# A graph layer that gathers its node rows: one tile of sixteen is picked by TensorE from rows kept in SBUF

## Chip, cores and metric

The kernel runs on one core of one Trainium2 chip. The metric is the device time of one execution in microseconds (us), here the median of three runs. The profile is of one further execution.

## What is computed

The program is two layers of a graph network over 8192 nodes of 128 f32 values and 262,144 edges sorted by `dst`, each layer followed by a residual sum and a layer norm. The change lies in the second layer, in which each edge takes the row of its source node, multiplies it with its nine attributes in a tensor product with fixed coefficients and learned weights, and is summed into its target node:

```python
x = _layernorm(x + _L0_gnn_ref(x, src, dst, edge_weight, L0_gnn_W))
# second layer, edge_index = (src, dst), edge_attr = edge_attr_9 (262144, 9)
summand = _tensor_product(x[src], edge_attr, [w0, w1, w2, w3, w4])   # (262144, 128)
out = segment_sum(summand, dst, num_segments=8192) / sqrt(10.0)
x = _layernorm(x + out)
```

## The kernel before

After the first layer and its norm the node rows lie in DRAM as `x1`. The second layer (`layer1`) walks the edges in 128 rows of 16 tiles of 128 edges. Each engine has a program of its own, written out by hand, and they meet at semaphores.

- **POOL** (GpSimd) gathers: for each tile one indirect DMA fetches the 128 source rows of `x1` into `feat[z][:, t, :]`, edge by edge on the partitions. `feat` has two slots of a row each (`ROW_SLOTS` is 2), and each slot two halves of 8 tiles; before a half of row r is gathered POOL waits until PE has used that half of row r - 2 (`half_summed`).
- **DVE** (VectorE) makes `attr_hot` for row r + 2 in row r (`next_hots`, `hots`): a comparison of a ramp (`iota`) with the target nodes gives a one-hot of 16 nodes for each edge, and a product with the nine attributes 9 x 16 columns for each tile. The one-hot and the ramp lie in PSUM in a corner of `y` (`loop_hot`, `loop_iota`) for rows 0 to 113; the one-hots made in rows 112 to 125, for which `y` is needed otherwise, use `late_hot` and the constants in SBUF. DVE also adds `quad` into `group` (`add_quads`, half by half) and the mixed sums into `g.acc` (`add_pair`).
- **PE** (TensorE) multiplies, in `half_row`, 8 tiles of `feat` with their `attr_hot` into the PSUM tile `quad`; after every second row `mix` applies the weights to `group` (nine products of 384 columns). Products of f32 operands show as two matmul records each. `turn_attr` turns the attributes of the next 8 rows (an octet) onto the edges' partitions.
- **ACT** (ScalarE) clears `quad` and `group`, copies the turned attributes and casts the indices. **SP** loads attributes.

Rows 0 to 7 stand in a first piece, 8 to 111 in a loop over octets, and 112 to 127 are written out, since in 112 to 126 the finished batches of 512 nodes are also turned (`turn_nodes`), summed with `x1`, measured and normalized (`measure`, `normalize`) and stored. The last batch follows behind row 127.

The order in one row of the loop is this on DVE (names as in the code below):

```python
add_quads(w, r, n, j // 2 % 2, j % 2, 0, offs)
if starts:
    add_pair(n - 1, starts)
add_quads(w, r, n, j // 2 % 2, j % 2, 1, offs)
next_hots(o, j)
```

Of the kernel before, what the change touches and what calls it, by code (L numbers as in the profile page):

```python
# [36 lines left out]
P = 128  # L37
# [7 lines left out]
TABLES = 1  # L45
# [47 lines left out]
START_LAG = 3  # L93
BATCH = 4
# [84 lines left out]
def gnn_kernel(nc, x, src, dst, attr, weight, w_lin, w_tp, consts, out, tables, x1):  # L179
# [10 lines left out]
    with ExitStack() as ctx:  # L190
# [31 lines left out]
        layer1(nc, g, x1, attr, out)  # L222
# [1197 lines left out]
def layer1(nc, g, x1, attr, out):  # L1420
# [5 lines left out]
    with ExitStack() as ctx:  # L1426
# [6 lines left out]
        off_f = sb("off_f", [P, TN], F32)  # L1433
        tile_offs = sb("tile_offs", [P, TN // Q, Q - 1], I32)
# [6 lines left out]
        late_hot = sb("late_hot", [P, R, WIN], F32)  # L1441
# [8 lines left out]
        x_t = [sb(f"x_t{i}", [P, BATCH, D], F32) for i in range(2)]  # L1450
        z_t = [sb(f"z_t{i}", [P, BATCH, D], F32) for i in range(2)]
        x_last = sb("x_last", [P, BATCH, D], F32)
        z_last = sb("z_last", [P, BATCH, D], F32)
# [6 lines left out]
        LOOPED = EARLY // O  # L1460

# [21 lines left out]
        x_used = sem("x_used")  # L1483
        y_made = sem("y_made")
# [23 lines left out]
        def in_slot(w, e):  # L1508

            return w * ((NE + 1 - e % 2) // 2) + e // 2  # L1510

# [8 lines left out]
        def _(sp):  # L1520
# [7 lines left out]
            sp.wait_ge(attr_turned, 2)  # L1528
            load_attr(1)

            def load_x(w, e):

                sp.wait_ge(x_used, w * NE + max(e + 1, 2))
                sp.dma_start(x_t[e % 2][:], batches(x1)[e]).then_inc(x_here[e % 2], 16)

            sp.dma_start(x_last[:], batches(x1)[NE]).then_inc(x_last_here, 16)
            with passes(sp) as w:
                with sp.Fori(0, LOOPED) as o:
                    sp.wait_ge(attr_turned, w * (2 * OCTETS) + o * 2 + 4)
                    load_attr(o + 2)  # L1540
                load_x(w, 0)
                for r in range(EARLY, RN):
                    if r % O == TURN_ROW + 1:
                        sp.wait_ge(attr_turned, w * (2 * OCTETS) + (r // O * 2 + 4))
# [3 lines left out]
            n_loads = sp.value_load(g.n_pass[0:1, 1:2], min_val=1, max_val=g.PASSES1)  # L1548
            sp.wait_ge(attr_here, n_loads * (16 * OCTETS) + 32)
# [3 lines left out]
        def _(pool):  # L1553
            with passes(pool) as w:
                with pool.Fori(0, OCTETS) as o:  # L1555
                    for j in range(O):
                        z = j % S
                        if j % (O // 2) == 0:
                            pool.wait_ge(ids_made, w * (2 * OCTETS) + o * 2 + (j // (O // 2) + 1))  # L1559
                        for h in range(2):  # L1560
                            pool.wait_ge(half_summed, summed(w, o * O, (j - S) * 2 + h))  # L1561
                            pool.sem_inc(g.turn, 1)  # L1562
                            for t in range(h * H, h * H + H):
                                c = j % (O // 2) * R + t
                                pool.indirect_dma_start(  # L1565
                                    feat[z][:, t, :], None, x1,
                                    bass.IndirectOffsetOnAxis(ap=ids[j // (O // 2)][:, c:c + 1], axis=0),
                                ).then_inc(feat_in[z][h], 16)
                for z in range(S):
                    for h in range(2):  # L1570
# [442 lines left out]
```

## Time and profile before

| | |
|---|---|
| median of 3 runs | 4139.94 us (4139.83 to 4140.0) |
| profiled execution, its own time | 4139.79 us |
| its span, first to last instruction | 4138.0 us |
| busy: PE / DVE / ACT / POOL | 2400.2 / 2119.9 / 1420.4 / 2769.7 us |
| gathers of the second layer (L1565) | 2048, 1960.3 us busy, mean 957 ns |
| mean granted TensorE clock | 0.749 |

The busy time of an engine is the sum of its instructions; "idle before" is the time in which the engine did nothing ahead of them, with what ended it. "issue" is idle time that nothing in the profile explains. L1565 is line 1565 of the kernel. A granted clock of 1.00 is 2.4 GHz, of 0.50 is 1.2 GHz.

### The profile page before, as it was taken

What the parts mean: (1) busy time and instruction counts of PE and PEld (TensorE: products, weight loads), DVE (VectorE), ACT (ScalarE), POOL (GpSimd) and SP (SyncE); (2) the same over time, 40 slices, a digit from 0 to 9 for tenths busy, and PEclk for the clock granted to TensorE, in tenths of its full rate; (3) what the DMA queues carried; (4) which work ended last, traced back from release to release, by engine and by line L of the source; (5) the groups of instructions that cost most, each with busy time, mean ns of one, the idle gap of its engine ahead of it and who ended that gap; (6) DMA issues with size and microseconds to landing.
All of it is one profiled execution on the core that took longest, in us unless ns stands there. A gap on an engine that the chain in (4) does not pass through costs nothing.

```text
span 4138.0 us, 55255 instructions
## 1 busy us (share of the span) xinstructions
PE 2400.2 (58%) x15332; PEld 2126.9 (51%) x15334; DVE 2119.9 (51%) x4357; ACT 1420.4 (34%) x2142; POOL 2769.7 (67%) x2887
## 2 busy tenths in 40 slices
PE   2200199999999964555455554545555455555454
PEld 1000199999999954444444444444444444444443
DVE  8999888888888872232222332322332222323433
ACT  5444366666666651121121211211121111212222
POOL 5100077777777737777777777777777777777775
PEclk6555599999999966677776776767667766776767
DMA  1000133333333332221221222222221221212222
GB/s 58 8 0 20 63 97 96 97 96 98 96 96 92 96 115 59 53 59 53 58 58 53 58 58 53 58 58 53 58 58 53 58 58 52 58 53 73 79 75 57
DMA packets 116447, 268.24 MB, mean 65 GB/s; under 512 B 50449, under 2 KB 50593, under 8 KB 115233
## 3 DMA queue, kind: packets, MB, share of 16 engines
q0 software_dynamic: 92080, 191.02, 17.4%
q1 hardware_dynamic: 19698, 68.09, 4.7%
q10 hardware_dynamic: 4608, 8.39, 0.5%
q8 instruction: 28, 0.46, 0.0%
q14 instruction: 33, 0.27, 0.0%
HBM read 252.30 MB, written 8.72 MB: 63 GB/s over the span
## 4 chain that ended last, share of the span: by engine, by line
POOL 42%; issue 16%; PE 4%; DMA 1%; POOLq 0%; DVE 0%; ACT 0%; DVEq 0%
POOL feat L1565 42%; PE quad L1730 3%; PE mixed L1742 1%; DMA feat<-x,ids 1%; POOLq L1561 0%; POOLq L1562 0%; PE attr_t L1690 0%; ACT z_last L1669 0%; DVE group L1878 0%; DVE dst_col L1965 0%; POOLq L1555 0%; DVE z_last L1976 0%; DVE stats L1979 0%; PE y L1754 0%; POOLq L1559 0%
## 5 line engine op out<-in xcount | busy, mean ns | idle before, releaser
L1565 POOL DMA_INDIRECT feat<-x,ids x2048 | 1960.3, 957 | 636.3 <-issue 632.3
L1730 PE MATMUL quad<-attr_hot,feat 128*128 128x144 f32 x4096 | 919.8, 407 | 1229.4 <-DMA feat<-x,ids 644.3
L1730 PEld LDWEIGHTS quad<-attr_hot,feat 128*128 128x128 f32 x4096 | 860.5, 294 | 1292.9 <-issue 1286.6
L1878 DVE TENSOR_TENSOR group<-group,quad 128x504 f32 (+1 forms) x512 | 347.9, 679 | 1725.5 <-PE quad L1730 1681.5
L1137 POOL DMA_INDIRECT l_feat<-in_x,id_of x768 | 727.7, 948 | 601.7 <-ACT w_of L830 366.4
L1582 ACT ACTIVATE quad<-quad 128x1008 uint32<-128x1008 uint32 x258 | 256.6, 995 | 1834.0 <-DVE group L1878 1834.0
L1742 PE MATMUL mixed<-group,mix 128*128 128x384 f32 x1152 | 414.9, 518 | 17.9 <-DVE group L1878 17.9
L1039 DVE TENSOR_SCALAR keys<-swap,src_of,w_of 128x184 f32<-128x184 f32 x1024 | 327.1, 389 | 93.5 <-PE l_pre L1230 93.5
L1039 DVE TENSOR_SCALAR w_row<-swap,src_of,w_of 128x184 f32<-128x184 f32 x1024 | 327.6, 390 | 51.4 <-PE l_pre L1230 49.7
L1742 PEld LDWEIGHTS mixed<-group,mix 128*128 128x128 f32 x1152 | 235.4, 209 | 171.7 <-issue 49.5
L1211 PE MATMUL got<-x_near,far_w 128*128 128x128 bf16 x4224 | 301.0, 220 | 11.0 <-ACT far_w L847 11.0
L1854 DVE TENSOR_TENSOR attr_hot<-y,attr_e 128x2304 f32<-128x2304 f32 x114 | 291.5, 2557 | 3.9
L1211 PEld LDWEIGHTS got<-x_near,far_w 128*128 128x128 bf16 x4224 | 272.4, 98 | 26.0 <-issue 11.3
L856 ACT COPY pad<-got 128x640 f32<-128x640 f32 x256 | 177.2, 692 | 291.0 <-PE got L1211 245.2
L1586 ACT ACTIVATE group<-group 128x3456 uint32<-128x3456 uint32 x66 | 203.4, 3083 | 193.4 <-PE mixed L1742 193.4
L1230 PE MATMUL l_pre<-keys,pad 128*128 128x184 f32 x1280 | 262.5, 319 | 0.0
L1230 PE MATMUL l_pre<-w_row,pad 128*128 128x184 f32 x1280 | 262.1, 319 | 0.0
L842 ACT ACTIVATE far_keys<-place,turn_f 128x384 bf16<-128x384 bf16 (+2 forms) x384 | 229.4, 631 | 7.0 <-DMA place<-table 6.9
L1230 PEld LDWEIGHTS l_pre<-keys,pad 128*128 128x128 f32 x1280 | 213.1, 190 | 0.0
L1230 PEld LDWEIGHTS l_pre<-w_row,pad 128*128 128x128 f32 x1280 | 212.6, 190 | 0.0
L1230 PE MATMUL l_pre<-keys,l_feat 128*128 128x184 f32 x768 | 189.9, 329 | 0.0
L1230 PE MATMUL l_pre<-w_row,l_feat 128*128 128x184 f32 x768 | 189.4, 328 | 0.0
(252 smaller groups left out, 2428.7 us busy)
## 6 DMA issues: line engine op xcount, KB each, us to landing
place<-table SPq DMA_DIRECT2D x64, 640.0 KB
feat<-x,ids POOLq DMA_INDIRECT x2048, 2.5
l_feat<-in_x,id_of POOLq DMA_INDIRECT x768
attr_in<-in_edge_attr SPq DMA_DIRECT2D x18, 576.0 KB, 3.8
norm_x<-in_x SPq DMA_DIRECT2D x16, 256.0 KB, 2.7
x<-norm_z ACTq DMA_DIRECT2D x16, 256.0 KB, 2.4
x_t<-x SPq DMA_DIRECT2D x15, 256.0 KB, 2.7
out<-z_t ACTq DMA_DIRECT2D x15, 256.0 KB, 2.1
```

What stands on the lines that cost most here:

```text
L842: nc.scalar.activation(rest_far[r][:, cols[r]], placed_at(s, j, cols[r]), ACT.Abs, bias=not_wanted[r]).then_inc(far_made, 2 // len(cols))
L1039: made = nc.vector.tensor_scalar(hot_of[(j % 2) * GROUP + i], iota[KIND[j][i]], src_of[s % 2][:, c:c + 1], w_of[s % 2][:, c:c + 1], ALU.is ...
L1137: pool.indirect_dma_start(feat[:, landing, :], None, x, bass.IndirectOffsetOnAxis(ap=id_of[s % 2][:, c:c + 1], axis=0)).then_inc(feat_in[l ...
L1211: last = nc.tensor.matmul(got[z][:, cols], hot, rows, start=(n_done == 0), stop=(n_done == len(products) - 1))
L1230: made = nc.tensor.matmul(pre[:, s % 2, bass.ds(places[i], WIN0)], rows, hot_of[(j % 2) * GROUP + i], start=False, stop=(j == GROUPS - 1 a ...
L1565: pool.indirect_dma_start(feat[z][:, t, :], None, x1, bass.IndirectOffsetOnAxis(ap=ids[j // (O // 2)][:, c:c + 1], axis=0),).then_inc(feat ...
L1582: nc.scalar.memzero(quad[:, 2 * h:2 * h + 2, 0:NA * QUAD_WIN]).then_inc(quad_zero, 1)
L1586: nc.scalar.memzero(group[n % 2][:]).then_inc(group_zero, 1)
L1730: last = nc.tensor.matmul(bank[:, :, bass.ds(places[t % H], WIN)], feat[z % S][:, t, :], attr_hot[z % 2][:, t, :, :], start=False, stop=(t ...
L1742: last = nc.tensor.matmul(to, g.mix[:, m, :], group[side][:, m, :, :], start=(m == 0), stop=(m == NA - 1))
L1854: nc.vector.tensor_tensor(attr_hot[z][:], hot.unsqueeze(2).to_broadcast(s4), by_tile.unsqueeze(3).to_broadcast(s4), ALU.mult).then_inc(hot ...
L1878: nc.vector.tensor_tensor(to, to, quad[:, q, 0:NA * QUAD_WIN].rearrange("p (m n) -> p m n", m=NA), ALU.add).then_inc(quad_added, 1)
```

## The change

In rows 16 to 112 tile 15 of each row is no longer gathered; POOL issues 8 gathers for the first half and 7 for the second. Its 128 node rows are picked on the chip:

- In rows 0 to 7 all node rows of `x1` are loaded in 16 batches and split into three bf16 parts whose sum is the f32 value, which stay in SBUF (`x3`, 64 blocks of 128 nodes x 3 x 128). ACT makes a part by a cast (`split_part`), PE subtracts it in PSUM with an identity and a negated identity (`keep_left`).
- Before row 0 DVE writes two numbers for each edge of the 128 last tiles (`src` modulo 128, and its block plus 1), which SP stores and then, four rows ahead, loads row by row onto all partitions (`load_codes`).
- In row r DVE compares them for the tile of row r + 2: `shift_codes` (four operations of 128 columns) and `block_hots`, two bursts of 8 comparisons of 512 bf16 columns each, which write `pick_hot`, a one-hot of 64 blocks x 128 edges.
- PE multiplies the 64 blocks of `pick_hot` with the 64 blocks of `x3` in `pick`, 32 behind each half of a row, into 384 columns of `y` (`picked`); DVE sums the three parts into tile 15 of the row after (`take_picked`).
- The one-hots of the edges and their ramp get a PSUM bank of their own (`hots_at`) for all rows; `attr_t` shrinks from two banks to one, so the attributes are turned in three steps, not two. `late_hot`, `z_t`, `x_last` and `z_last` go; the batches are normalized in `x_t`, which lies in the memory of `pick_hot`.

```diff
-        late_hot = sb("late_hot", [P, R, WIN], F32)
...
-        attr_t = ctx.enter_context(nc.psum_tensor("attr_t", [P, 2, 512], F32))
+        attr_t = ctx.enter_context(nc.psum_tensor("attr_t", [P, O // 2 * P], F32))
...
-        loop_hot = y[:, 0:R * WIN].rearrange("p (t n) -> p t n", t=R)
-        loop_iota = y[:, R * WIN:R * WIN + WIN]
...
+        hots_at = ctx.enter_context(nc.psum_tensor("hots_at", [P, 512], F32))
+        hot = hots_at[:, 0:R * WIN].rearrange("p (t n) -> p t n", t=R)
+        iota = hots_at[:, R * WIN:R * WIN + WIN]
...
+        x3 = sb("x3", [P, NODE_BLOCKS, 3, D], BF16)
+        pick_hot = sb("pick_hot", [P, NODE_BLOCKS, P], BF16)
+        code4 = sb("code4", [P, HOT_BLOCKS, P], BF16)
...
+        picked = y[:, 0:3 * D]
...
+        PICK = 2 * O
+        PICKS = EARLY + 1 - PICK
+        CODED = PICKS + 1
...
+            def load_codes(w, r, s):
+
+                sp.wait_ge(codes_used, coded(w, r - PICK) + 1)
+                sp.sem_inc(g.turn, 1)
+                sp.dma_start(codes_at[:, s, :], rows[bass.ds(r, 1)].to_broadcast([P, P])).then_inc(codes_here[s], 16)
...
+                    for h in range(2):
+                        pool.wait_ge(half_summed, summed(w, o * O, (j - S) * 2 + h))
+                        pool.sem_inc(g.turn, 1)
+                        for t in range(h * H, h * H + (second if h else H)):
+                            c = j % (O // 2) * R + t
+                            pool.indirect_dma_start(
+                                feat[z][:, t, :], None, x1,
+                                bass.IndirectOffsetOnAxis(ap=ids[j // (O // 2)][:, c:c + 1], axis=0),
+                            ).then_inc(feat_in[z][h], 16)
...
+                with pool.Fori(2, LOOPED) as o:
+                    for j in range(O):
+                        gather_row(o, j, H - 1)
+                for r in range(EARLY, RN):
+                    gather_row(r // O, r % O, second_half(r))
...
+            def split_part(w, b, part):
+
+                if part == 0:
+                    act.wait_ge(x_here[b % 2], split_load(w, b) * 16 + 16)
+                    rows = x_t[b % 2]
+                else:
+                    act.wait_ge(left_made, w * (2 * g.NB) + (2 * b + part))
+                    rows = y[:].rearrange("p (a d) -> p a d", a=BATCH)
+                nc.scalar.copy(x3[:, b * BATCH:(b + 1) * BATCH, part, :], rows).then_inc(split, 1)
...
+            def keep_left(w, b):
+
+                rows = y[:].rearrange("p (a d) -> p a d", a=BATCH)
+                for part in range(2):
+                    pe.wait_ge(split, w * (3 * g.NB) + (3 * b + part + 1))
+                    if part == 0:
+                        nc.tensor.matmul(rows, g.cst[:, C_IDENT:C_IDENT + P], x_t[b % 2], start=True, stop=False,
+                                         skip_group_check=True)
+                    nc.tensor.matmul(rows, minus, x3[:, b * BATCH:(b + 1) * BATCH, part, :], start=False, stop=True,
+                                     skip_group_check=True).then_inc(left_made, 1)
+
+            def pick(w, k, half):
+
+                pe.wait_ge(pick_hots, coded(w, k) * 2 + (half + 1))
+                if half == 0:
+                    pe.wait_ge(pick_out, picks_done(w, k) + 1)
+                pe.sem_inc(g.turn, 1)
+                for b in range(half * (NODE_BLOCKS // 2), (half + 1) * (NODE_BLOCKS // 2)):
+                    last = nc.tensor.matmul(picked, pick_hot[:, b, :], x3[:, b, :, :].rearrange("p c d -> p (c d)"),
+                                            start=(b == 0), stop=(b == NODE_BLOCKS - 1), skip_group_check=True)
+                last.then_inc(pick_made, 1)
...
+                if with_pick is not None:
+                    pe.wait_ge(pick_out, picks_done(w, with_pick) + 2)
...
+                    half_row(w, r, 0, j, fills * H)
+                    turn_rest(w * OCTETS + o + 1, j)
+                    if first:
+                        keep_left(w, 2 * j)
+                    if pick_next:
+                        pick(w, r - (PICK - 1), 0)
+                    half_row(w, r, 1, j, n_second, r - PICK if with_pick else None)
+                    if first:
+                        keep_left(w, 2 * j + 1)
+                    if pick_next:
+                        pick(w, r - (PICK - 1), 1)
...
+            def shift_codes(w, i, s, n_slot):
+
+                dve.wait_ge(codes_here[s], n_slot * 16 + 16)
+                nc.vector.scalar_tensor_tensor(code4[:, 0, :], codes[:, s, 0, :], g.cst[:, C_PLACE:C_PLACE + 1],
+                                               codes[:, s, 1, :], ALU.is_equal, ALU.mult).then_inc(codes_used, 1)
+                dve.wait_ge(codes_used, coded(w, i) + (CODE_SLOTS + 1))
+                for k in range(1, HOT_BLOCKS):
+                    nc.vector.tensor_scalar(code4[:, k, :], code4[:, 0, :], float(k), None,
+                                            ALU.subtract).then_inc(code_shifted, 1)
+                dve.wait_ge(code_shifted, coded(w, i) * (HOT_BLOCKS - 1) + (HOT_BLOCKS - 1))
+
+            def block_hots(half):
+
+                n = NODE_BLOCKS // 2 // HOT_BLOCKS
+                for b in range(half * n, (half + 1) * n):
+                    made = nc.vector.tensor_scalar(pick_hot[:, b * HOT_BLOCKS:(b + 1) * HOT_BLOCKS, :], code4[:],
+                                                   float(b * HOT_BLOCKS + 1), None, ALU.is_equal)
+                made.then_inc(pick_hots, 1)
+
+            def take_picked(w, k, z):
+
+                dve.wait_ge(pick_made, picks_done(w, k) * 2 + 2)
+                nc.vector.tensor_reduce(feat[z][:, R - 1, :], picked.rearrange("p (c d) -> p d c", c=3), AX_X,
+                                        ALU.add).then_inc(pick_out, 1)
...
+                    if code_next:
+                        i = r - (PICK - 2)
+                        s = (j + 2) % CODE_SLOTS
+                        n_slot = coded_in_slot(w, s) + o * (O // CODE_SLOTS) + ((j + 2) // CODE_SLOTS - PICK // CODE_SLOTS)
+                        dve.wait_ge(split, (w + 1) * (3 * g.NB))
+                        if take_next:
+                            dve.wait_ge(pick_made, picks_done(w, r - (PICK - 1)) * 2 + 1)
+                        shift_codes(w, i, s, n_slot)
+                        block_hots(0)
                     add_quads(w, r, n, j // 2 % 2, j % 2, 1, offs)
                     next_hots(o, j)
+                    if take_next:
+                        take_picked(w, r - (PICK - 1), (j + 1) % S)
+                    if code_next:
+                        block_hots(1)
```

The diff leaves out the loads and stores around the codes, the table work before row 0, and the late rows. Two places show how the engines' programs read now. The first is DVE in one row of the loop; before, from the first half's adds (L1878) to the one-hots of row r + 2:

```order
L1878 TENSOR_TENSOR group<-group,quad 128x9x56
L1871 REGISTER_ALU
L1874 REGISTER_ALU
...
L1878 TENSOR_TENSOR group<-group,quad 128x9x56
L1849 REGISTER_ALU
L1850 TENSOR_TENSOR y<-y,dst_col 128x256
L1854 TENSOR_TENSOR attr_hot<-y,attr_e 128x2304
L1859 TENSOR_LOAD row_offs
```

And of the change at the same place (L2075 are the adds, L2090 and L2094 the codes' shifts, L2102 the bursts, L2109 the sum of the parts; `code` is `code4`, and `tile_start` holds the codes):

```order
L2075 TENSOR_TENSOR group<-group,quad 128x9x56
...
L2090 SCALAR_TENSOR_TENSOR code<-tile_start,cst 128x128
L2094 TENSOR_SCALAR code<-code 128x128 x3
L2102 TENSOR_SCALAR pick_hot<-code 128x512 x8
L2068 REGISTER_ALU
...
L2075 TENSOR_TENSOR group<-group,quad 128x9x56
L2047 TENSOR_TENSOR hots_at<-hots_at,dst_col 128x256
L2051 TENSOR_TENSOR attr_hot<-hots_at,attr_e 128x2304
L2108 REGISTER_ALU
L2109 TENSOR_REDUCE feat<-y 128x128
L2102 TENSOR_SCALAR pick_hot<-code 128x512 x8
```

The first burst now stands between the two halves' adds, the second behind the one-hots.

The second place is PE in the same rows; before, from the last tile of a first half (L1730) to the first of the second:

```order
L1730 MATMUL quad<-attr_hot,feat 128x9x16
L1713 ISA
L1713 TENSOR_LOAD tile_offs
L1723 REGISTER_ALU
L1730 MATMUL quad<-attr_hot,feat 128x9x16
```

And of the change, where the quad matmuls are L1900 and the pick is L1883 (`x` is `x3`):

```order
L1900 MATMUL quad<-attr_hot,feat 128x9x16
L1878 ISA
L1880 ISA
L1883 MATMUL y<-x,pick_hot 128x384 x32
L1859 ISA
L1859 TENSOR_LOAD tile_start
L1891 REGISTER_ALU
```

Between the halves, and behind the second one in the same way, 32 matmuls of the pick now stand in PE's program.

## Rows read from the trace of the kernel before

**Rows 1.** Page, part 2: busy tenths in 40 equal slices of the span

```profile
POOL 5100077777777737777777777777777777777775
```

**Rows 2.** Groups by line, 1600 to 3600 us (count | busy us, mean ns | idle before, releasers)

```profile
L1565 POOL DMA_INDIRECT feat<-x,ids x1602 | 1512.4, 944 | 488.1 <-issue 486.2 <-PE quad L1730 1.8
...
L1878 DVE TENSOR_TENSOR group<-group,quad 128x504 f32 x300 | 203.9, 680 | 926.6 <-PE quad L1730 890.3 <-issue 8.0
...
L1600 ACT COPY attr_e<-attr_t 128x512 f32<-128x512 f32 x26 | 14.0, 589 | 25.2 <-DVE attr_hot L1854 25.2
```

**Rows 3.** Windows, 2000 to 2400 us (busy us of PE, PEld, DVE, ACT, POOL; clock)

```profile
2000.00:2400.00 400.00, 205.48 (x836) 171.66 (x835) 118.35 (x141) 74.08 (x64) 302.51 (x321) 0.70 0.21 56
```

**Rows 4.** Waits of POOL, 1600 to 3600 us (total us, times, longest)

```profile
POOL feat L1565 <- PE quad L1730: 1.8, 6, 0.3
```

**Rows 5.** Timeline, POOL: first and last gather of the layer (start, duration)

```profile
1529.47 2.17 POOL L1565 DMA_INDIRECT feat<-x,ids  x1 [12.63 <-issue]
...
4112.46 0.94 POOL L1565 DMA_INDIRECT feat<-x,ids  x1 [0.30 <-issue]
```

**Rows 6.** Page, part 5: all gathers of the second layer

```profile
L1565 POOL DMA_INDIRECT feat<-x,ids x2048 | 1960.3, 957 | 636.3 <-issue 632.3
```

**Rows 7.** Groups by line, 3810 to 4130 us

```profile
L1565 POOL DMA_INDIRECT feat<-x,ids x226 | 235.7, 1043 | 68.9 <-issue 67.9 <-PE quad L1730 0.6 <-DMA feat<-x,ids 0.3
```

**Rows 8.** Timeline, a late row at 3883 us

```profile
3883.37 2.56 DVE L1854 TENSOR_TENSOR attr_hot<-late_hot,attr_e 128x2304 f32<-128x2304 f32 x1
3883.72 3.03 POOL L1565 DMA_INDIRECT feat<-x,ids  x1 [0.30 <-issue]
```

**Rows 9.** Timeline, the start of the second layer

```profile
1531.94 1.29 POOL L1565 DMA_INDIRECT feat<-x,ids  x1 [0.30 <-issue]
...
1534.04 1.50 DVE L1833 TENSOR_SCALAR off_f<-tile_start,keep 128x2048 f32<-128x2048 f32 x1
1534.79 1.55 POOL L1565 DMA_INDIRECT feat<-x,ids  x1 [0.30 <-issue]
...
1536.65 2.03 POOL L1565 DMA_INDIRECT feat<-x,ids  x1 [0.30 <-issue]
```

**Rows 10.** Timeline, first layer: a burst of comparisons and a gather

```profile
510.95 0.32 DVE L1029 TENSOR_SCALAR far_w<-place,cst 128x384 bf16<-128x384 bf16 x1 [7.11 <-DMA place<-table]
...
511.18 0.31 DVE L1030 TENSOR_SCALAR far_w<-place,cst 128x384 bf16<-128x384 bf16 x1
511.33 0.98 POOL L1137 DMA_INDIRECT l_feat<-in_x,id_of  x1 [0.30 <-issue]
511.41 0.31 DVE L1029 TENSOR_SCALAR far_w<-place,cst 128x384 bf16<-128x384 bf16 x1
511.64 0.31 DVE L1030 TENSOR_SCALAR far_w<-place,cst 128x384 bf16<-128x384 bf16 x1
```

**Rows 11.** Line 1137, gathers of the first layer, 700 to 1400 us (min/median/max ns)

```profile
L1137 POOL DMA_INDIRECT l_feat<-in_x,id_of x560: 940/945/1050, 699.5 to 1399.6; - x187
```

**Rows 12.** Line 1159, f32 matmuls of 512 columns (min/median/max ns)

```profile
L1159 PE MATMUL got<-l_feat,cst x24: 1061/1126/1223, 59.8 to 214.6; 128*128 128x512 f32 x24
```

**Rows 13.** Timeline, PE: half rows and a mix

```profile
1544.05 4.18 PE L1730 MATMUL quad<-attr_hot,feat 128*128 128x144 f32 x16 [5.89 <-DMA feat<-x,ids]
...
1597.60 5.97 PE L1742 MATMUL mixed<-group,mix 128*128 128x384 f32 x18
...
1604.09 2.20 PE L1730 MATMUL quad<-attr_hot,feat 128*128 128x144 f32 x16 [0.41 <-issue]
...
4085.80 2.12 PE L1730 MATMUL quad<-attr_hot,feat 128*128 128x144 f32 x16
```

**Rows 14.** Timeline, first layer, PE: matmuls of 128 bf16 columns

```profile
1005.97 1.00 PE L1211 MATMUL got<-x_near,far_w 128*128 128x128 bf16 x15
...
1006.80 0.22 PE L1211 MATMUL got<-x_rest,far_w 128*128 128x128 bf16 x1
```

**Rows 15.** Windows, first layer, 800 to 900 us

```profile
800.00:900.00 100.00, 100.00 (x1003) 98.43 (x1002) 86.30 (x275) 67.33 (x136) 75.62 (x81) 1.00 0.32 98
```

More of the change, by code:

```diff
@@ L1483, in layer1 @@
         x_used = sem("x_used")
+        src_here = sem("src_here")
+        code_step = sem("code_step")
+        codes_made = sem("codes_made")
+        codes_stored = sem("codes_stored")
+        codes_here = [sem(f"codes_here{s}") for s in range(CODE_SLOTS)]
+        codes_used = sem("codes_used")
+        code_shifted = sem("code_shifted")
+        split = sem("x_split")
+        left_made = sem("x_left_made")
+        pick_hots = sem("pick_hots")
+        pick_made = sem("pick_made")
+        pick_out = sem("pick_out")
         y_made = sem("y_made")
@@ new lines, in _ @@
+                with pool.Fori(0, 2) as o:
+                    for j in range(O):
+                        gather_row(o, j, H)
+                with pool.Fori(2, LOOPED) as o:
+                    for j in range(O):
+                        gather_row(o, j, H - 1)
+                for r in range(EARLY, RN):
+                    gather_row(r // O, r % O, second_half(r))
+                landings = [16 * n for z in range(S) for n in (H * (RN // S), landed_before(RN + z))]
+                for landing, n in zip(sum(feat_in, []), landings):
+                    pool.wait_ge(landing, n)
@@ L1610, in normalize @@
                 for a in range(BATCH):
[L1611 removed]
+                    done = nc.scalar.activation(x_t[e % 2][:, a, :], x_t[e % 2][:, a, :], ACT.Identity,
                                                 bias=shift[:, a:a + 1], scale=rstd[:, a:a + 1])
@@ L1668, in _ @@
             for a in range(BATCH):
-                done = nc.scalar.activation(z_last[:, a, :], z_last[:, a, :], ACT.Identity, bias=shift[:, a:a + 1],
+                done = nc.scalar.activation(x_last[:, a, :], x_last[:, a, :], ACT.Identity, bias=shift[:, a:a + 1],
                                             scale=rstd[:, a:a + 1])
@@ L1689, in turn_attr @@
                 for n, m in enumerate(ms):
-                    last = nc.tensor.transpose(attr_t[:, n // 4, n % 4 * P:(n % 4 + 1) * P], edges[:, :, m],
+                    last = nc.tensor.transpose(attr_t[:, n * P:(n + 1) * P], edges[:, :, m],
                                                g.cst[:, C_IDENT:C_IDENT + P])
@@ L1773, in _ @@
                 pe.wait_ge(landings_cleared, w + 1)
+                pe.wait_ge(x_used, w * NE + 2)
                 pe.sem_inc(g.turn, 1)
                 for j in range(O):
-                    row(0, j, first=True)
-                with pe.Fori(1, LOOPED) as o:
+                    row(0, j, first=True, pick_next=False, with_pick=False)
+                for j in range(O):
+                    row(1, j, pick_next=(j == O - 1), with_pick=False)
+                with pe.Fori(2, LOOPED) as o:
                     for j in range(O):
@@ L1840, in _, with hots @@
             dve.sem_inc(hot_made, 1)
-            def hots(u, r, j, z, late=False):
-                hot = late_hot[:] if late else loop_hot
-                iota = g.cst[:, C_IOTA:C_IOTA + WIN] if late else loop_iota
+            nc.vector.tensor_copy(iota, g.cst[:, C_IOTA:C_IOTA + WIN]).then_inc(iota_made, 1)
+            dve.wait_ge(iota_made, 1)
+            dve.wait_ge(src_here, 16)
+            nc.vector.tensor_scalar(low_i, src_tail, P - 1, None, ALU.bitwise_and).then_inc(code_step, 1)
+            nc.vector.tensor_scalar(block_i, src_tail, 7, NODE_BLOCKS - 1, ALU.logical_shift_right,
+                                    ALU.bitwise_and).then_inc(code_step, 1)
+            dve.wait_ge(code_step, 2)
+            nc.vector.tensor_copy(code_out[:, 0, :], low_i)
+            nc.vector.tensor_copy(block_f, block_i).then_inc(code_step, 1)
+            dve.wait_ge(code_step, 3)
+            nc.vector.tensor_scalar(code_out[:, 1, :], block_f, 1.0, None, ALU.add).then_inc(codes_made, 1)
+            def hots(u, r, j, z):
                 cols = bass.ds(r * R, R)
@@ L1946, in _ @@
                 for j in range(O):
-                    row(0, j, first=True)
-                with dve.Fori(1, LOOPED) as o:
+                    row(0, j, first=True, code_next=False, take_next=False)
+                for j in range(O):
+                    row(1, j, code_next=(j >= O - 2), take_next=(j == O - 1))
+                with dve.Fori(2, LOOPED) as o:
                     for j in range(O):
```

231 lines of the change are left out of this document (148 added, 83 removed).

## Prediction

> **What bounds the kernel now.** I read the page's slices first [rows 1]. The second layer fills the last 25 of the 40 slices; there POOL stands at 7 tenths in all but the last, where the kernel ends. The groups by line over 1600 to 3600 us [rows 2] say what POOL's 7 tenths are: 1602 gathers with 1512.4 us busy and 488.1 us idle before them, which is 2000.5 of 2000 us. So POOL issues one gather every 1.249 us (0.944 busy, 0.305 "issue") without a pause, and a row of 16 takes 19.98 us. The waits [rows 4] confirm that nothing holds it: it waited for PE 6 times, 1.8 us in all. The window [rows 3] shows the room elsewhere: in 400 us, twenty rows, PE is busy 205 us (10.3 a row) and DVE 118 us (5.9 a row), with TensorE granted 0.70 of its clock.
>
> The second layer is therefore one POOL stream. Its first gather starts at 1529.47 and its last ends at 4113.40 [rows 5]; 24.6 us of tail follow to the end of the span at 4138.0. The profiled run took 4139.79 us, 1.8 us more than its span and 0.15 us less than the median of the three runs.
>
> The stream is not quite even. Over all 2048 gathers POOL is busy 1960.3 us [rows 6], against 2048 x 0.944 = 1933.3 at the middle's duration: 27.0 us of lengthened gathers. They lie at the two ends. In the last rows the mean is 1043 ns [rows 7], since a gather that starts under the product for `attr_hot`, which there reads `late_hot` and `attr_e`, both in SBUF, lasts until 0.8 us after that product ends [rows 8] (3883.37 + 2.56 = 3885.93; the gather ends at 3886.75). At the start of the layer single-source work on long SBUF tiles does the same [rows 9] (the scalar product ends at 1535.54, the gather at 1536.34). So a gather needs something that DVE holds, once, some 0.13 us after its start (0.94 - 0.81).
>
> **The change, part by part.**
>
> *Gathers removed.* Rows 16 to 112 are 97 rows with one gather less: 97 x 1.249 = 121.1 us off the stream. The gathers that stay keep their duration and their "issue" gap; nothing in POOL's program between them changes.
>
> *One-hots in their own bank.* The late product now reads its one-hot from PSUM, as the middle rows do, where no gather is longer than 0.95 us. Of the 27.0 us the first gather [rows 5] and three others of the start [rows 9] hold 3.3 (2.17 + 1.29 + 1.55 + 2.03 less 4 x 0.944); 23.7 us remain for the late rows and go. The last 226 gathers alone give 235.7 - 226 x 0.944 = 22.4 [rows 7], and they leave out one of the fourteen rows concerned.
>
> *DVE's one-hots of the nodes.* A row adds two bursts of 8 comparisons, bf16 128x512 from SBUF to SBUF, four small operations before the first burst, and a reduction of 384 PSUM columns. The nearest rows are the first layer's comparisons, 128x384 bf16, which start every 0.23 us in a burst [rows 10]. For 512 columns that is between 0.23 and 0.31; I take 0.27, so 2.1 us a burst, 4.3 a row. With about 0.9 for the small ones and at most 0.68 for the reduction (an add of 504 PSUM columns [rows 2]) DVE goes from 5.9 to about 11.8 us a row, of 18.7. It is not the bound. Behind its waits for the picks stand the second half's adds and the one-hots of row r + 2; PE needs those a row later.
>
> *What the bursts do to the gathers.* A gather that starts amid a burst of four such comparisons took 0.98 us in place of 0.94 [rows 10], and over 700 us of the first layer, with DVE busy some 86% [rows 15] with such short operations, 560 gathers had a median of 945 and a maximum of 1050 ns [rows 11]. So a short comparison delays a gather by its own few hundredths at most, and POOL gets in between two of them. A row has 4.3 / 1.249 = 3.4 gathers under a burst: 3.4 x 0.04 = 0.14 us a row, 13 us in all. The bounds are 0 and, at the maximum of 0.105 each, 35 us.
>
> The Trainium skill has a rule that speaks against this change (SBUF — State Buffer, section "Who interferes with whom"): single-source copies and tensor_scalar operations in SBUF can run in a two-port mode, and then hold the port pair that VectorE shares with GpSimd for the whole instruction, while the other engine is fully blocked. For a long instruction the trace agrees [rows 9]. Taken of a whole burst the rule would give the 4286 us of the second rival below, where the rows of short instructions [rows 10, 11] give 4008.
>
> *PE.* This is the change's real cost. A pick is 64 matmuls of 384 bf16 columns. In the first layer 15 matmuls of 128 bf16 columns, weights loaded anew for each, take 1.00 us [rows 14], one alone 0.22: (1.00 - 0.22) / 14 = 0.056 us each. Three times that is 0.167, and 10.7 us a pick. Half a row of tiles takes 2.12 to 2.20 at the high clock and 4.18 at the low; a mix every second row 5.97 after a half row that had raised the clock [rows 13]. Two rows at the high clock: 4 x 2.12 + 5.97 + 2 x 10.7 + 0.5 of transposes (9 x 128 columns in 8 rows, as many as a half row has) = 36.4 us, against POOL's 2 x 15 x 1.249 = 37.5. PE fits, with 1.1 us to spare in two rows. At the low clock it would need twice that, far beyond POOL. Which level holds? Of the 255 half rows that the trace shows whole, all 63 that began within 0.6 us of earlier PE work ran at the high clock (2.12 to 2.20), while the other 192, after 4.5 us idle or more, began at the low one [rows 13] (the first of each kind, and the last of the 63); and where PE is busy 100% the granted clock is 1.00 (2.4 GHz) for 100 us on end [rows 15]. With PE busy 97% I take the high level.
>
> Do the waits cost PE anything? A half row waits for its gathers, as now. The picks of PE's row r use one-hots that DVE made in row r - 1, and the reduction of the pick before has to be done when a pick begins: when a pick ends DVE may still have the edges' one-hots in hand (2.56 us [rows 8] and a short comparison before it) and then the reduction, while PE has a half row of 2.1 and perhaps a mix to do first, and the adds and one-hots were begun during the pick's 5.3. POOL runs almost two rows ahead of PE (two buffers), so a late PE of a few us costs nothing as long as the average fits.
>
> *Work hidden.* In rows 0 to 7 ACT and PE split the node rows: a half row of tiles (4.18), an identity matmul of 512 f32 columns in two passes of 1.13 [rows 12], three copies of 512 columns (0.59 each, as the copy from `attr_t` [rows 2]) and two bf16 products (0.45 each: 4 x 0.056, doubled for the low clock) follow each other: about 4.2 + 2.3 + 1.8 + 0.9 = 9.2 us a half row of POOL's 10.0. With a mix every second row (3.0 a row) that is 21.4 against 20.0: a lag of at most 1.4 us a row, 11 over eight rows. It lies under POOL's lead, since POOL needs half a buffer back only 24 gathers (30 us) after it filled it; without that cover it would cost the 11 us. On SP the next octet's attributes now stand behind the codes' loads, which wait until DVE has used a slot four rows before; the attributes are wanted several rows later still, and the third turning of them lies between PE's waits. None of this touches POOL's queue.
>
> **Sum**, against the profile's own span: 4138.0 - 121.1 - 23.7 + 13 = 4006.2 us; with the 1.8 around it **4008 us**, 3.2% faster. Its own range is 3990 to 4040 (the gathers' bounds are 3995 and 4030).
>
> **Rivals.**
> *PE becomes the bound.* For it: only 1.1 us of room in two rows, and no row shows a restart after 0.6 to 4.5 us of idle time, which is just what PE will have. Against it: a PE that is late has no gap, so its clock stays up; the loss limits itself. If each gap cost a cold start of 4.18 - 2.12 = 2.06 us, two rows would take 36.4 + 2 x 2.06 = 40.5, as long as now, and the 121 us would be lost. Half way lies 4008 + 60 = **4070 us**. A DVE that waits for PE and PE for it in turn would look alike.
>
> *The bursts starve POOL: slower.* If a burst of back-to-back comparisons held a gather until its end, each burst of 2.1 us would catch one gather, 0.62 us in on average, and delay it by 1.5 us: 3.0 a row, 291 us in 97 rows, less the 13 in the sum: **4286 us**. It decides from 0.75 us a burst on, where the gain (1.249 a row and 23.7 / 97 = 0.24) is eaten. For it: one long instruction does just that [rows 8, 9]. Against it: the gather at 511.33 would then have ended near 512.75, and ended at 512.31 [rows 10].
>
> *The late rows keep their stalls*, since other work of those rows (the batches' normalization) holds the gathers: 4008 + 24 = **4032 us**. Against it: a late gather ends 0.82 us after the product [rows 8], which explains its length whole.
>
> **Chances.** Forecast (3990 to 4040) 0.70; late stalls stay 0.05; PE or DVE bound 0.16, evenly from 4030 to 4135; starved POOL, slower, 0.06; something else 0.03. Up to 4080 about 0.83 is held, so the range is 3990 to 4080. A measurement of this kernel tells about 0.2% (8 us) from no change. Faster by more: 0.89; within it, the far end of PE as the bound: 0.03; slower: 0.08.
>
> **What would show it.** POOL 1951 gathers, still one every 1.25 us, mean near 0.95, waits for PE below 10 us; 18.7 to 18.9 us a row between rows 16 and 112; PE above 90% busy there at a clock near 1.0; no gather of 3 us in the late rows. POOL waiting for PE's half rows, or a clock near 0.7 in that stretch, means the first rival; gathers of 2 us beside the bursts, the second. The prediction is wrong if a pick matmul takes more than 0.18 us in a stream, or if a gather beside a burst loses more than 0.1.

## The result, and the profile after

The changed kernel takes **4013.07 us** (median of 4 runs, 4010.54 to 4014.28) against 4139.89 us before: a ratio of 0.9693, 95% interval 0.9678 to 0.9709, 3.1% faster. The forecast was 4008 us, range 3990 to 4080. The profiled execution took 4012.53 us, its span 4010.7.

From the page of the changed kernel, the share of each engine, the slices of PE, DVE, POOL and TensorE's granted clock, and the costliest groups of the second layer (L1668 are now the gathers, L1883 the pick, L2102 the bursts):

```profile
PE 3135.9 (78%) x21605; PEld 2469.3 (62%) x21606; DVE 2613.2 (65%) x6420; ACT 1446.3 (36%) x2190; POOL 2671.5 (67%) x2790
...
PE   2100189999999995657999999999999999998555
...
DVE  8999878888888874225565555555555555655443
...
POOL 5100077777777756777777777777777777777775
PEclk6555599999999986868999999999999999999777
...
L1668 POOL DMA_INDIRECT feat<-x,ids x1951 | 1862.3, 955 | 606.9 <-issue 585.5
...
L2102 DVE TENSOR_SCALAR pick_hot<-code 128x512 bf16<-128x512 bf16 x1568 | 371.9, 307 | 3.4
```

POOL's row of sevens is the one of [rows 1]: the second layer is still one stream of gathers, 97 fewer. PE has gone from half its time (205 of 400 us, [rows 3]) to 9 tenths without becoming the bound, and its granted clock has risen from 0.70 to 0.99 in these rows.

The groups of the picked rows, 1900 to 3600 us, answer to [rows 2]:

```profile
L1668 POOL DMA_INDIRECT feat<-x,ids x1350 | 1289.5, 955 | 411.4 <-issue 392.5 <-PE quad L1900 18.9
...
L1900 PE MATMUL quad<-attr_hot,feat 128*128 128x144 f32 x2880 | 395.9, 292 | 109.8 <-DMA feat<-x,ids 87.8 <-issue 22.0
```

1350 gathers are 90 rows of 15, so a row takes 1700 / 90 = 18.89 us, and a gather 1.259 where 1.249 was forecast. POOL's busy and idle time add up to 1700.9 us. The 18.9 us put down to PE are the usual gap between two gathers and no hold: POOL's waits for PE in these rows (us in total, times, longest) are at most 0.3 us long.

```profile
POOL feat L1668 <- PE quad L1900: 18.9, 62, 0.3
```

PE's half rows wait for gathers (87.8 us): POOL leads, PE follows.

Two windows of 400 us (busy us of PE, PEld, DVE, ACT, POOL; clock; DMA share) answer to [rows 3]:

```profile
1900.00:2300.00 400.00, 374.29 (x2238) 257.03 (x2238) 231.38 (x596) 77.75 (x69) 303.30 (x318) 0.99 0.24 61
...
3100.00:3500.00 400.00, 373.96 (x2262) 257.44 (x2261) 233.22 (x602) 78.74 (x70) 303.40 (x318) 1.00 0.24 61
```

PE is busy 94%, 17.7 us of a row's 18.89, at 2.4 GHz nearly throughout. The timeline shows one burst, its gathers, a half row and a pick:

```profile
2504.91 0.94 POOL L1668 DMA_INDIRECT feat<-x,ids  x1 [0.30 <-issue]
...
2505.41 1.89 DVE L2102 TENSOR_SCALAR pick_hot<-code 128x512 bf16<-128x512 bf16 x8
2506.16 1.02 POOL L1668 DMA_INDIRECT feat<-x,ids  x1 [0.30 <-issue]
...
2506.29 2.20 PE L1900 MATMUL quad<-attr_hot,feat 128*128 128x144 f32 x16 [1.39 <-DMA feat<-x,ids]
2507.49 0.94 POOL L1668 DMA_INDIRECT feat<-x,ids  x1 [0.30 <-issue]
...
2508.32 5.36 PE L1883 MATMUL y<-x,pick_hot 128*128 128x384 bf16 x32
```

The gather at 2506.16 starts under a burst and takes 1.02 us; the one after it takes 0.94 again. The gather at 2504.91 started before the burst and isn't lengthened, though the burst begins while it runs. PE's half row begins after 1.39 us of idle time and still runs at the high clock (2.20 us; 4.18 at the low one, [rows 13]).

At the two ends of the layer, the first gathers and the last, the last mix, and the group of the late rows, 3690 to 4010 us, which answers to [rows 7]:

```profile
1528.12 1.88 POOL L1668 DMA_INDIRECT feat<-x,ids  x1 [12.62 <-issue]
1530.30 1.56 POOL L1668 DMA_INDIRECT feat<-x,ids  x1 [0.30 <-issue]
1532.16 2.03 POOL L1668 DMA_INDIRECT feat<-x,ids  x1 [0.30 <-issue]
1534.50 2.48 POOL L1668 DMA_INDIRECT feat<-x,ids  x1 [0.30 <-issue]
...
3983.75 0.94 POOL L1668 DMA_INDIRECT feat<-x,ids  x1 [0.30 <-issue]
...
3992.49 7.74 PE L1912 MATMUL mixed<-group,mix 128*128 128x384 f32 x18 [1.99 <-DVE group L2075]
...
L1668 POOL DMA_INDIRECT feat<-x,ids x237 | 223.6, 943 | 72.2 <-issue 71.6 <-PE quad L1900 0.6
```

No late gather is lengthened any more: a mean of 943 ns where it was 1043, and the longest takes 961.

### The profile page after: what moved, and what is told of

It reads as the page before. It is cut to its first block, busy times and chain, and to the rows that moved or that the text cites. A ratio compares the mean times of both kernels' runs of the same rounds, so it can differ in the third digit from the quotient of the medians.

```text
span 4010.7 us, 71536 instructions
## 1 busy us (share of the span) xinstructions
PE 3135.9 (78%) x21605; PEld 2469.3 (62%) x21606; DVE 2613.2 (65%) x6420; ACT 1446.3 (36%) x2190; POOL 2671.5 (67%) x2790
## 4 chain that ended last, share of the span: by engine, by line
POOL 40%; issue 14%; PE 4%; DMA 3%; POOLq 0%; DVE 0%; ACT 0%; DVEq 0%
POOL feat L1668 40%; PE quad L1900 4%; DMA feat<-x,ids 3%; PE mixed L1912 0%; POOLq L1664 0%; POOLq L1665 0%; ACT pick_hot L1807 0%; DVE group L2075 0%; DVE dst_col L2199 0%; POOLq L1676 0%; PE attr_t L1829 0%; DVE pick_hot L2210 0%; DVE stats L2213 0%; DVE acc L2084 0%; POOLq L1574 0%
## 5 line engine op out<-in xcount | busy, mean ns | idle before, releaser
L1668 POOL DMA_INDIRECT feat<-x,ids x1951 | 1862.3, 955 | 606.9 <-issue 585.5
L1883 PE MATMUL y<-x,pick_hot 128*128 128x384 bf16 x6208 | 1044.3, 327 | 0.0
L1900 PE MATMUL quad<-attr_hot,feat 128*128 128x144 f32 x4096 | 643.9, 318 | 353.5 <-DMA feat<-x,ids 184.1
L1900 PEld LDWEIGHTS quad<-attr_hot,feat 128*128 128x128 f32 x4096 | 606.1, 216 | 413.0 <-issue 398.8
L1883 PEld LDWEIGHTS y<-x,pick_hot 128*128 128x128 bf16 x6208 | 609.2, 98 | 383.6 <-issue 3.9
L2075 DVE TENSOR_TENSOR group<-group,quad 128x504 f32 (+1 forms) x512 | 347.3, 678 | 735.3 <-PE quad L1900 698.8
L1912 PE MATMUL mixed<-group,mix 128*128 128x384 f32 x1152 | 395.1, 499 | 16.1 <-DVE group L2075 16.1
L2102 DVE TENSOR_SCALAR pick_hot<-code 128x512 bf16<-128x512 bf16 x1568 | 371.9, 307 | 3.4
L2051 DVE TENSOR_TENSOR attr_hot<-hots_at,attr_e 128x2304 f32<-128x2304 f32 x128 | 327.3, 2557 | 4.4
L1912 PEld LDWEIGHTS mixed<-group,mix 128*128 128x128 f32 x1152 | 222.7, 196 | 163.9 <-issue 30.2
L2090 DVE SCALAR_TENSOR_TENSOR code<-tile_start,cst 128x128 bf16<-128x128 bf16 x98 | 34.5, 352 | 331.8 <-PE y L1883 328.8
```

What stands on the lines that cost most here:

```text
L1668: pool.indirect_dma_start(feat[z][:, t, :], None, x1, bass.IndirectOffsetOnAxis(ap=ids[j // (O // 2)][:, c:c + 1], axis=0),).then_inc(feat ...
L1883: last = nc.tensor.matmul(picked, pick_hot[:, b, :], x3[:, b, :, :].rearrange("p c d -> p (c d)"), start=(b == 0), stop=(b == NODE_BLOCKS ...
L1900: last = nc.tensor.matmul(bank[:, :, bass.ds(places[t % H], WIN)], feat[z % S][:, t, :], attr_hot[z % 2][:, t, :, :], start=False, stop=(t ...
L1912: last = nc.tensor.matmul(to, g.mix[:, m, :], group[side][:, m, :, :], start=(m == 0), stop=(m == NA - 1))
L2051: nc.vector.tensor_tensor(attr_hot[z][:], hot.unsqueeze(2).to_broadcast(s4), by_tile.unsqueeze(3).to_broadcast(s4), ALU.mult).then_inc(hot ...
L2075: nc.vector.tensor_tensor(to, to, quad[:, q, 0:NA * QUAD_WIN].rearrange("p (m n) -> p m n", m=NA), ALU.add).then_inc(quad_added, 1)
```

## The experiments

Eleven kernels ran. Each is compared with the kernel before on its own chip; there that one took 4138.81 us (the bank, no bursts, less work for PE), 4141.85 (the doubled bursts, the two with more work for PE, the codes in PSUM) and 4139.51 (the last four). Except where said, an edit is to the changed kernel.

**The bank without the pick.** All gathers are back, nothing is picked; the split of the node rows and the one-hots' own bank stay.

```diff
-            return H - 1 if PICK <= r < PICK + PICKS else H
+            return H
...
-                def row(o, j, first=False, code_next=True, take_next=True):
+                def row(o, j, first=False, code_next=False, take_next=False):
```

> The one-hots in their own bank and the split of the node rows stay; nothing is picked, so all 2048 tiles are gathered and the codes are neither loaded nor shifted. My account: the late rows' lengthened gathers go and nothing else changes: the time before less 23.7 us, 4116 us (4112 to 4120), and gathers of the late rows at a mean of 944 to 950 ns. If other work of the late rows holds the gathers, 4135 to 4140 us and a mean near 1043 ns there. If the split of the node rows costs POOL time, above 4120 us, with POOL waiting for PE in rows 0 to 9.

Measured: 4116.33 us (ratio 0.9945, 0.9928 to 0.9962). Its gathers between 3800 and 4090 us:

```profile
L1660 POOL DMA_INDIRECT feat<-x,ids x232 | 218.9, 944 | 70.7 <-issue 70.1 <-PE quad L1892 0.6
```

The bank alone gives 22 to 24 us, all of the 23.7 put down to the late rows, so the split of the node rows, which is in this kernel too, costs nothing that can be measured; POOL's waits for PE in its second layer are at most 0.3 us long. The picks account for the other 4116.3 - 4013.1 = 103 us.

**The picks without the bursts.** `pick_hot` is made for the first picked row only.

```diff
+                if again:
+                    dve.sem_inc(pick_hots, 1)
+                    return
```

> The two bursts of comparisons are run for the first picked row alone; in the other 96 rows PE multiplies with the same one-hots, so that tile 15 of these rows gets the nodes of row 16 (left out: the one-hots of rows 17 to 112). PE's work and the gathers are the same. My account: the 16 us by which gathers beside bursts are longer go, 4013 - 16 = 3997 us (3994 to 4000), and the gathers of these rows have a mean of 944 to 946 ns. If the lengthening comes of DVE's other work (the edges' one-hots, the adds): 4011 to 4014 us. If the chain of DVE's bursts and PE's picks sets the row: also below 4000, but with the gathers' mean unchanged and fewer waits of POOL for PE.

Measured: 3996.79 us (0.9657, 0.9641 to 0.9673). The gathers from 1900 to 3600 us:

```profile
L1668 POOL DMA_INDIRECT feat<-x,ids x1362 | 1285.8, 944 | 415.1 <-issue 397.1 <-PE quad L1900 18.0
```

So the bursts cost 4013.1 - 3996.8 = 16.3 us (15 by the two ratios), and the gathers' own duration holds all of it: 11 ns x 15 x 97 = 16.

**The bursts doubled.** Each comparison is issued a second time.

```diff
+                for again in range(2):
+                    for b in range(half * n, (half + 1) * n):
...
+                    if not again:
+                        made.then_inc(hots_once, 1)
+                        dve.wait_ge(hots_once, i * 2 + (half + 1))
```

> Each burst of 8 comparisons is issued twice, the second time behind a wait for the first; DVE goes from 10.9 to about 14.6 us a row. Without bursts the time was 3996.8 us, with them 4013.1, so they cost 16.3. My account (a gather amid short comparisons loses what is left of one, some 0.085 us, however long the burst): twice the cost, 4013 + 16 = 4029 us (4024 to 4036), and a mean of the gathers near 966 ns in rows 16 to 112. If a burst holds a gather until it ends: each burst of 3.8 us catches one gather and delays it by about 3.2 us where it now delays it by 1.3, far above 4150 us. If the chain of DVE and PE sets the row: POOL waits for PE, up to 4013 + 97 x 3.7 = 4370 us.

Measured: 4037.14 us (0.9749, 0.9733 to 0.9765), one us above the range. The gathers from 1900 to 3600 us, and the timeline of one doubled burst:

```profile
L1669 POOL DMA_INDIRECT feat<-x,ids x1334 | 1294.5, 970 | 406.6 <-issue 386.4 <-PE quad L1901 20.1
...
2506.86 3.88 DVE L2104 TENSOR_SCALAR pick_hot<-code 128x512 bf16<-128x512 bf16 x16
2506.93 1.04 POOL L1669 DMA_INDIRECT feat<-x,ids  x1 [0.30 <-issue]
2508.28 1.03 POOL L1669 DMA_INDIRECT feat<-x,ids  x1 [0.30 <-issue]
2509.61 1.02 POOL L1669 DMA_INDIRECT feat<-x,ids  x1 [0.30 <-issue]
2510.93 0.94 POOL L1669 DMA_INDIRECT feat<-x,ids  x1 [0.30 <-issue]
```

Three gathers lie under it, each about 0.09 us longer, and none waits for the burst's end; that ends the starvation rival. The bursts' cost went from 16 to about 37 us (4037.1 - 3996.8, less the 3.0 by which the kernel before ran longer on this chip; by the means 26 ns x 15 x 97 = 38), more than double. The timelines show why: between 1900 and 3600 us 192 of 1350 gathers took 0.97 us or more (hits) in the changed kernel, 2.13 a row, and 423 of 1334 here, 4.76 a row; a hit costs 0.080 there and 0.083 here. The price of a hit is constant, their number grew a little faster than the bursts.

**Less work for PE.** The pick leaves out the third part.

```diff
-        picked = y[:, 0:3 * D]
+        picked = y[:, 0:2 * D]
```

> PE picks two of the three parts, 256 columns a matmul instead of 384 (left out: the third part, so a picked row has 16 bits of its value's 24). That takes 64 x 0.054 = 3.5 us a row from PE. My account: POOL's stream sets the row, so nothing moves: 4013 us (4010 to 4016). If PE sets it: the row falls to POOL's own 15 x 1.249 = 18.74 us, 0.15 us less, 3998 us. If the longer pauses let the clock fall to its low level: half rows of 4.2 us and matmuls of 0.22 us, PE at 7.3 x 2 + 14 = 28 us a row, far above 4100 us, unless the clock comes back.

Measured: 4017.1 us (0.9707, 0.9691 to 0.9723), one us above the range. Its window, and its gathers from 1900 to 3600 us:

```profile
1900.00:2300.00 400.00, 330.38 (x2236) 278.55 (x2237) 228.71 (x597) 77.76 (x69) 303.39 (x318) 0.92 0.23 61
...
L1668 POOL DMA_INDIRECT feat<-x,ids x1347 | 1289.7, 957 | 410.5 <-issue 393.4 <-PE quad L1900 17.1
```

With a third less pick PE's busy time falls by 44 of 374 us, and nothing is gained: PE is not the bound. With the longer pauses the mean clock is 0.92 where it was 0.99: of 179 half rows seen whole between 1900 and 3600 us 57 took more than 2.25 us, some of them 4.18; the remaining 122 took the 2.1 to 2.2 of the high level. The gathers' mean is 957 ns, 2 more than without this edit. DVE starts a burst behind a pick, so PE's new rhythm puts the bursts elsewhere: by the timelines a burst covers the moment 0.13 us after a gather's start 3.28 times a row here, 2.78 times in the changed kernel.

**More work for PE.** 4, and in a second kernel 16, matmuls of 384 columns more for each pick.

```diff
+                for b in range(16 if half == 0 else 0):
+                    nc.tensor.matmul(picked, pick_hot[:, b, :], x3[:, b, :, :].rearrange("p c d -> p (c d)"),
+                                     start=True, stop=True, skip_group_check=True)
```

> Ahead of each pick PE does 4 more matmuls of 384 columns, which the pick overwrites: 4 x 0.1625 = 0.65 us a row, 18.3 us in all. My account: less than POOL's 18.9, so the time stays: 4013 us (4010 to 4018). If PE is the bound already: 97 x 0.65 = 63 us, 4076 us.

> Ahead of each pick PE does 16 more matmuls of 384 columns, which the pick overwrites: 16 x 0.1625 = 2.6 us a row. PE is busy 374 of 400 us in these rows, 17.7 us of a row's 18.9. My account: PE, off the path now, becomes the bound: 17.7 + 2.6 = 20.3 us a row, 1.4 more than now, 97 x 1.4 = 136 us, 4149 us (4120 to 4165), with POOL waiting for PE. If PE is the bound already: 97 x 2.6 = 252 us, 4265 us. If PE has over 2.6 us of room: 4013 us.

Measured: 4019.97 us with 4 (0.9708, 0.9692 to 0.9725) and 4138.23 us with 16 (0.9989, 0.9980 to 0.9999). The gathers of both from 1900 to 3600 us, first with 4:

```profile
L1668 POOL DMA_INDIRECT feat<-x,ids x1346 | 1291.6, 960 | 410.3 <-issue 396.3 <-PE quad L1903 14.0
```

Then with 16, with POOL's waits for PE (us in total, times, longest) and a window of that kernel:

```profile
L1668 POOL DMA_INDIRECT feat<-x,ids x1264 | 1209.8, 957 | 491.1 <-issue 391.9 <-PE quad L1903 99.2
POOL feat L1668 <- PE quad L1903: 99.2, 59, 4.4
...
1900.00:2300.00 400.00, 395.45 (x2399) 270.90 (x2398) 214.54 (x557) 73.25 (x63) 295.18 (x309) 0.99 0.21 58
```

With 4 POOL is still held by nothing; the 5 to 7 us more (the kernel before ran 2 us longer on this chip), 2 above the range, go with the gathers' mean of 960 ns, 5 more in 15 x 97 gathers, 7 us. With 16 PE is the bound: busy 99%, a row takes 1700 / (1264 / 15) = 20.17 us, POOL waits for PE up to 4.4 us at a time, and the whole gain is gone. This is what the first rival looks like, and it begins somewhere between 18.3 and 20.3 us of PE's work a row (17.7 and the 0.65 or 2.6 added).

**The codes in PSUM.** The bursts read f32 codes from the rest of the one-hots' bank, two blocks at a time; the ramp moves to SBUF for it.

```diff
-HOT_BLOCKS = 4
+HOT_BLOCKS = 2
...
-        iota = hots_at[:, R * WIN:R * WIN + WIN]
+        iota = g.cst[:, C_IOTA:C_IOTA + WIN]
...
-        code4 = sb("code4", [P, HOT_BLOCKS, P], BF16)
+        code4 = hots_at[:, R * WIN:512].rearrange("p (k e) -> p k e", k=HOT_BLOCKS)
```

> The codes that the bursts compare lie in PSUM, as f32, two blocks at a time instead of four, so a burst is 16 comparisons of 256 columns from PSUM to SBUF; the edges' ramp is read from SBUF instead. If only work from SBUF to SBUF holds a gather, the 16 us go: 3997 to 4000 us with a gather mean of 944 to 947 ns. DVE's comparisons get longer, 32 x about 0.35 = 11.2 us a row where they now take 3.8 (from the adds of 504 PSUM columns, 0.68 us), 18.3 us a row of POOL's 18.7; if that or the later picks hold PE, POOL waits for PE and the time is above 4020 us, with a gather mean that still tells about the port. If any DVE instruction beside a gather delays it, the mean stays at 955 ns or rises.

Measured: 4001.25 us (0.9661, 0.9645 to 0.9677), one us above the range. Gathers and bursts, 1900 to 3600 us, and a window:

```profile
L1668 POOL DMA_INDIRECT feat<-x,ids x1359 | 1286.0, 946 | 414.2 <-issue 395.6 <-PE quad L1900 18.6
L2102 DVE TENSOR_SCALAR pick_hot<-hots_at 128x256 bf16<-128x256 f32 x2896 | 974.5, 411 | 3.1
...
1900.00:2300.00 400.00, 375.19 (x2249) 255.92 (x2247) 374.46 (x894) 79.10 (x71) 302.72 (x320) 1.00 0.22 62
```

The 16 comparisons of a burst now last 5.4 us, almost three times as long, DVE is busy 374 of 400 us, and the gathers are all but undisturbed (946 ns; 944 without bursts). It is not how long DVE works but where it reads from. A comparison is also half as wide here, 256 columns for 512; that was not tried alone.

**The codes as f32 in SBUF.**

```diff
-        code4 = sb("code4", [P, HOT_BLOCKS, P], BF16)
+        code4 = sb("code4", [P, HOT_BLOCKS, P], F32)
```

> The codes stay in SBUF, four blocks at a time, but as f32 instead of bf16, so the bursts compare f32 from SBUF with bf16 one-hots out to SBUF. With the codes in PSUM the mean of the gathers fell from 955 to 946 ns and the time by 12 us or more. If it is work from SBUF to SBUF that holds a gather, whatever its type, the gathers lose as much as now or more, by the comparisons' length: 4013 us or above, mean 955 ns or above. If only the bf16 comparisons hold a gather (a mode that f32 input doesn't run in), the mean falls to 944 to 947 ns and the time to 3997 to 4001 us, as long as DVE fits into the row.

Measured: 4052.1 us (0.9790, 0.9777 to 0.9803), beside 4013.28 us for the changed kernel on the same chip. Gathers and bursts from 1900 to 3600 us:

```profile
L1668 POOL DMA_INDIRECT feat<-x,ids x1322 | 1298.7, 982 | 402.9 <-issue 392.2 <-PE quad L1900 10.7
L2102 DVE TENSOR_SCALAR pick_hot<-code 128x512 bf16<-128x512 f32 x1408 | 509.6, 432 | 3.0
```

A burst of 8 takes 2.9 us in place of 1.9, 4.27 gathers a row are hit, and a hit costs 0.135 us in place of 0.080. So f32 holds a gather too; longer comparisons hold it longer.

The Trainium skill bears on this (SBUF — State Buffer, section "Who interferes with whom"): a VectorE operation with at most one SBUF input, outside the two-port modes, doesn't contend with GpSimd, while one in such a mode does, and the first of the two to issue holds the shared ports for its whole instruction. The codes in PSUM agree, with 946 ns; the codes in SBUF agree, with 955 and 982, if their comparisons run in such a mode, which no run here shows by itself. That a burst of such instructions lets GpSimd in between two of them is what the doubled burst adds.

**Picks from row 12 on, alone and with the codes in PSUM.** Edits: `PICK = O + CODE_SLOTS`, the rows of the second octet written out on POOL, and the conditions of SP's, PE's and DVE's rows to match. With them ran the changed kernel once more.

> The changed kernel once more, for the comparison on the same chip: 4013 us (4010 to 4018).

> The picks begin at row 12 instead of row 16 (PICK = O + CODE_SLOTS), so four gathers more are left out, 1947 in all. My account: 4 x 1.249 = 5.0 us off the stream, less 4 x 0.165 for the bursts: 4.3 us less than the changed kernel on the same chip. If the split of the node rows, which ends in row 7, is late for row 10's first burst, POOL waits for PE in rows 10 to 14 and the gain is gone or turned over: the changed kernel's time or some us above.

> Both: codes in PSUM as f32, two blocks at a time, and picks from row 12 on. If the two gains add up: the kernel with the codes in PSUM took 4001 us, and 4 x 1.249 = 5.0 us go: 3996 us (3993 to 4000).

Measured, in this order: 4013.28 us (0.9697, 0.9683 to 0.9710), 4009.81 us (0.9685, 0.9672 to 0.9698) and 3993.46 us (0.9648, 0.9635 to 0.9661). Four gathers less give 3.5 us alone, where 4.3 were expected. Both edits together beat the changed kernel by 19.8 us, 0.5%, with intervals that don't meet. The gathers of the combination, 1900 to 3600 us:

```profile
L1668 POOL DMA_INDIRECT feat<-x,ids x1361 | 1285.3, 944 | 415.7 <-issue 406.2 <-PE quad L1899 9.5
```

## Why the prediction was right

The mechanism held: one POOL stream, 97 gathers shorter, with PE just under it. The sum was 4006.2 us of span and the span is 4010.7:

| term | forecast | measured |
|---|---|---|
| gathers left out | 97 x 1.249 = -121.1 | 97 fewer; picks with their bursts -103, and the bursts' +16 apart: -119 to -120 |
| late stalls | -23.7 | -22 to -24 (the bank alone); late mean 943 ns |
| bursts on the gathers | +13 | (1289.5 - 1350 x 0.944) / 90 x 97 = +16.3 |
| four lengthened gathers at the start | unchanged (7.04 us) | 7.95 us: +0.9 |
| start of the stream | unchanged (1529.47) | 1528.12: -1.35 |
| tail behind the last gather | unchanged (24.6) | 4010.7 - 3984.69 = 26.0: +1.4 |
| the span's 4.5 us over the forecast | | 3.3 (bursts) + 0.9 - 1.35 + 1.4 = 4.3 |

From the start of its first gather to the end of its last the stream is 2456.6 us long, where it was 2583.9: 127.4 us less (131.8 were forecast), and the bursts and the four gathers make up 4.2 of the 4.4 between.

- **The bursts on the gathers** were near in the sum and wrong in both factors. "3.4 gathers under a burst, 0.04 each" became 2.13 a row that are hit, at 0.080. The 0.04 was read from a single gather [rows 10]. One factor was too high by 1.6 and the other too low by 2, so that the sum came within 3 us is luck; the bounds, 0 and 35 us, held the 16.
- **A burst** was put at 2.1 us and took 1.74 to 2.06, 1.88 in the median (0.226 us from comparison to comparison where I took 0.27); DVE is busy 10.9 us a row, not 11.8.
- **PE** was put at 36.4 us in two rows and was busy 374.29 / 400 x 37.78 = 35.35; half a pick took 5.36 us, so 10.7 a pick, as forecast. The level of the clock was right. "No row shows a restart after 0.6 to 4.5 us of idle time" is answered for pauses like the 1.39 us above: of 176 half rows seen whole between 1900 and 3600 us 68 began after more than 0.6 us of idle time and still ran at the high level, in 2.12 to 2.21 us. Six others, after 2.15 to 2.66 us, took 2.94 to 3.87. So the cold start that the first rival feared did occur, but rarely, and POOL did not wait for it.
- **The room of PE**: about 1.2 us a row by the windows, more than the forecast's 1.1 in two rows. 0.65 us more of work left POOL unheld; 2.6 us more made PE the bound.
- **The split in the first octet** was hidden, as said: with no picks at all the time is what the bank alone explains, and POOL's waits for PE in the whole layer of the changed kernel (us in total, times, longest) hold nothing longer than a usual gap:

```profile
POOL feat L1668 <- PE quad L1900: 21.3, 70, 0.3
```

  The forecast that these waits stay below 10 us missed that the profile puts some usual gaps down to PE without a hold.
- **The middle rows** before hold no gather longer than 0.961 us; the prediction read 0.95.
- **The tail** was not foreseen: the last mix took 7.74 us, where this stood in the same place before:

```profile
4121.19 6.04 PE L1742 MATMUL mixed<-group,mix 128*128 128x384 f32 x18 [1.99 <-DVE group L1878]
```

  The mean granted clock over that mix was 0.78, and 1.00 before, so it ran in part at the low level. What made the clock differ there, with a half row of 4.18 us and 1.99 us of idle time ahead of the mix in both kernels, stays open.

The three rivals fell: PE as the bound by the kernels with less and more of its work, starvation by the doubled bursts, the late stalls by the bank alone.

## What to carry to other kernels

Where one engine issues a stream without a pause, a change is worth its count times the stream's period, and what it adds elsewhere is free up to the next engine's room, unless it lengthens the stream's own instructions, as the bursts did; measure that room by adding dummy work until the time moves, as 0.65 and 2.6 us a row did here. Beside gathers from GpSimd, look at where VectorE's operands lie before looking at how long it works: a longer comparison from PSUM cost next to nothing here, a shorter one from SBUF 16 us. A price read from one row may be off by two and still give the right sum by luck; count hits and price apart.

## What was not expected of the hardware

- A gather that is held beside a burst of comparisons 0.226 us apart loses 0.08 us almost every time (192 hits, 0.080 on average, 182 of them 1.02 or 1.03 us long; 423 hits at 0.083 with bursts twice as long), with comparisons 0.35 us apart 0.135 (376 hits).
- Which gathers are hit goes by one moment, the 0.13 us after the start that the prediction worked out. In the changed kernel, 1900 to 3600 us, a burst covers that moment of 250 gathers, and 190 of them are hit; of the other 1100 it is 2.
- How many gathers are hit depends on the rhythm of PE: 2.13 a row in the changed kernel, 2.6 with 4 matmuls more or with two parts, and there the time was 4 to 7 us longer though PE was not the bound.
- A comparison of 256 f32 columns from PSUM took 0.41 us (started every 0.33 us), one of 512 bf16 columns from SBUF 0.31 (every 0.23).
